# A projection phase and an expert phase on one core: batch 0's attention chain issued one projection step sooner, two edits at the start, and fourteen filling matmuls taken out

## The reference, cut to what matters

```
h = layernorm(x) * (1 + ca) + sa
Q, K, V = h @ Wq.T + bq, h @ Wk.T + bk, h @ Wv.T + bv        # 16 heads of 16
Q, K = elu(Q) + 1, elu(K) + 1
KV, K_sum = einsum('bshd,bshe->bhde', K, V), K.sum(axis=1)    # over the whole batch
Z = 1 / (einsum('bshd,bhd->bsh', Q, K_sum) + 1e-06)
x = x + ga * (einsum('bshd,bhde,bsh->bshe', Q, KV, Z) @ Wo.T + bo)
h = layernorm(x) * (1 + cb) + sb
gates = softmax over the best 2 of 8 of (cosine(h, centroids) + h @ w_route.T)
x = x + gb * sum over experts of gates * (gelu(h @ w1 + b1) @ w2 + b2)
```

## Time and profile before

| | us |
|---|---|
| median of 3 runs | 363.19 (362.65 to 363.71) |
| the profiled execution, own time | 362.67 |
| its span | 360.9 |
| PE busy | 346.5 (96%) |
| DVE busy | 286.6 (79%) |
| POOL busy | 259.4 (72%) |
| ACT busy | 234.7 (65%) |

### The profile page before, as it was taken

One profiled execution on the slowest core, in us unless ns is written; L12 is line 12 of the kernel. 1 busy time (PEld: TensorE's weight loads), 2 busy tenths in 40 slices (PEclk: granted clock), 3 DMA queues, 4 the chain that ended last, 5 costly groups with the idle time before them and its releaser, 6 DMA issues.

```text
span 360.9 us, 8816 instructions
## 1 busy us (share of the span) xinstructions
PE 346.5 (96%) x2790; PEld 324.3 (90%) x2790; DVE 286.6 (79%) x819; ACT 234.7 (65%) x517; POOL 259.4 (72%) x358
## 2 busy tenths in 40 slices
PE   8899999998999988799999999999999999999995
PEld 8667888887888977799998999999999999999895
DVE  5589676658748889989999889898898888876754
ACT  4685878887877745756747476584574765855541
POOL 4367999977867587787897878988889867755210
PEclk9999999999999999999999999999999999999999
DMA  8953630000000033133242322421323214214311
GB/s 266 331 167 94 192 96 0 2 3 0 2 0 3 4 117 119 56 93 105 55 136 80 69 91 61 147 85 63 130 65 97 88 60 145 91 61 145 98 51 61
DMA packets 23715, 31.82 MB, mean 88 GB/s; under 512 B 2288, under 2 KB 14204, under 8 KB 23680
## 3 DMA queue, kind: packets, MB, share of 16 engines
q1 hardware_dynamic: 23240, 31.34, 28.2%
q10 hardware_dynamic: 440, 0.04, 0.1%
HBM read 27.04 MB, written 4.34 MB: 87 GB/s over the span
## 4 chain that ended last, share of the span: by engine, by line
PE 73%; DVE 17%; issue 4%; ACT 3%; DMA 1%; POOL 1%; DVEq 0%; ACTq 0%; POOLq 0%
PE bank L797 20%; PE bank L798 19%; PE bank L799 19%; PE bank L805 4%; PE bank L852 3%; DVE hid_g L1355 2%; PE bank L829 2%; PE bank L981 2%; DVE bank L1372 2%; DVE early L1272 1%; DVE gT_f L1411 1%; DVE den L1303 1%; PE bank L1023 1%; PE bank L908 1%; DVE qz_lo L1310 1%
## 5 line engine op out<-in xcount | busy, mean ns | idle before, releaser
L740 ACT ACTIVATE bank<-bank,cols_sb 128x256 f32<-128x256 f32 x128 | 51.3, 438 | 43.3 <-PE bank L799 43.0
L797 PE MATMUL bank<-tr_hi,w_hi 128*128 128x256 f32 x256 | 73.4, 287 | 0.0
L798 PE MATMUL bank<-tr_lo,w_hi 128*128 128x256 f32 x256 | 72.3, 282 | 0.0
L799 PE MATMUL bank<-tr_hi,w_lo 128*128 128x256 f32 x256 | 72.1, 282 | 0.0
L797 PE MATMUL bank<-w_hi,hid_pair 128*128 128x256 f32 x252 | 70.5, 280 | 0.0
L799 PE MATMUL bank<-w_hi,hid_pair 128*128 128x256 f32 x252 | 70.3, 279 | 0.0
L798 PE MATMUL bank<-w_lo,hid_pair 128*128 128x256 f32 x252 | 70.2, 279 | 0.0
L501 POOL TENSOR_TENSOR hid_pair<-hid_g,hid_pair 128x512 fp32r<-128x512 f32 x42 | 54.3, 1292 | 7.0 <-POOL gT_r L526 3.3
L797 PEld LDWEIGHTS bank<-tr_hi,w_hi 128*128 128x128 f32 x256 | 48.8, 191 | 0.3 <-DVE hid_g L1355 0.2
L799 PEld LDWEIGHTS bank<-tr_hi,w_lo 128*128 128x128 f32 x256 | 48.9, 191 | 0.0
L798 PEld LDWEIGHTS bank<-tr_lo,w_hi 128*128 128x128 f32 x256 | 48.8, 191 | 0.0
(11 more groups left out here) (162 smaller groups left out, 928.3 us busy)
## 6 DMA issues: line engine op xcount, KB each, us to landing
g_bc<-g_dram SPq DMA_DIRECT2D x64, 256.0 KB, 3.5
x_sb<-in_x SPq DMA_DIRECT2D x16, 256.0 KB, 3.0
out<-x_sb SPq DMA_DIRECT2D x15, 256.0 KB, 2.3
early<-in_wmod SPq DMA_DIRECT2D x3, 512.0 KB, 7.0
q_sb<-in_w SPq DMA_DIRECT2D x2, 512.0 KB, 6.5
q_sb<-in_w SPq DMA_DIRECT2D x1, 1024.0 KB, 9.5
mod_row<-mod_dram SPq DMA_DIRECT2D x1, 1024.0 KB, 6.2
q_sb<-in_wqkvT SPq DMA_DIRECT2D x2, 384.0 KB, 5.3
```

Source lines behind the costliest of these rows:

```text
L740: last = ac.activation(half, half, ACT.Gelu, bias=b1_sb[:, e:e + 1])
L797: te.matmul(out_ap, l_hi, r_hi, start=start, stop=False, skip_group_check=shared)
L798: te.matmul(out_ap, l_hi, r_lo, start=False, stop=False, skip_group_check=shared)
L799: return te.matmul(out_ap, l_lo, r_hi, start=False, stop=stop, skip_group_check=shared)
```

## The change

In words, engine by engine:

- Start: VectorE makes the low half of the bias row (`bqk_r`) ahead of unit 0's low half, not behind it. TensorE issues `v(0)` ahead of `tp_a(1)`.
- TensorE, projection phase: `sum_k(0)` from inside step 9 to the end of step 8; `make_m(0)` from inside step 11 to the end of step 10; `tp_o(0)` and `tp_o(1)` from steps 12 and 14 to 11 and 13; `attend(0)` and `attend(1)` from 13 and 15 to 12 and 14; `tp_e(0)` and `route(0)` from step 15 and behind it to step 14.
- The other engines move their parts of it in the same way. New in step 15 are, on VectorE, `gates_a(0)` ahead of the feature map of the first half of unit 15 and `gates_b(0)` between the two halves; on GpSimd `exp_gates(0)`, then `rstd_e(1)`, then `add_bo(7)`; on ScalarE `normalise_e(1)` ahead of `keep_v(15)`.
- Step -1: TensorE issues `first(0, 0)`, `kv(15)`, `first(0, 1)`, `tp_e(1)`, `first(0, 2)`, `tp_o(2)`, `first(0, 3)`, `attend(2)`, `sum_k(1)`, `route(1)`; both fills are gone. ScalarE does `square(1)` and `hi_e(1)` between the first two gelus. `tp_o(2)` now waits for unit 1's low half (`e_lo` one higher), since both use bank 0.

```diff
@@ POOL step_a
-                if u.nth(UPB + 6):
+                if u.nth(UPB + 5):
                     rstd_e(unit(0))
...
+                if u.nth(NU - 1):
+                    exp_gates(unit(0))
+                    rstd_e(unit(1))
+                    add_bo(unit(UPB - 1))
@@ ACT step_a
+                if u.nth(NU - 1):
+                    normalise_e(unit(1))
                 if u.plus(2):
                     normalise(u.plus(2))
-                if u.nth(UPB + 4):
-                    hi_o(unit(0))
                 keep_v(u)
@@ PE step_a
                 if u.nth(NU - 1):
                     kv(u.plus(-1))
                 v(u)
+                if u.nth(0):
+                    tp_a(u.plus(1))
                 if u.plus(-1) and not u.nth(NU - 1):
                     kv(u.plus(-1))
+                if u.nth(UPB):
+                    sum_k(0, bank[0][:, 0:E])
+                if u.nth(UPB + 2):
+                    make_m(0, bank[1])
+                if u.nth(UPB + 6):
+                    pe.wait_ge(route_ready, 1)
+                    route(unit(0))
@@ PE step_e
+                if u.nth(-1):
+                    first(u.plus(1), 1)
+                    tp_e(unit(1))
+                    first(u.plus(1), 2)
                 if u.plus(3):
                     tp_o(u.plus(3))
...
-                    fill(bank[6], 7)
@@ DVE, the start
+            dve.wait_ge(bqk_step, 2)
+            TT(bqk_r[32:33, :], bqk_raw[32:33, :], bqk_t[32:33, :].bitcast(F32), ALU.subtract).then_inc(bqk_ready, 1)
             dve.wait_ge(a_hi, 1)
             TT(tr_lo[:, 0, :, :], tr_f[:, 0, :, :], tr_hi[:, 0, :, :].bitcast(F32), ALU.subtract).then_inc(a_lo, 1)
@@ DVE step_a
                 if u.nth(NU - 1):
 
                     dve.wait_ge(w_ready, NU)
+                    gates_a(unit(0))
...
                 feature_map(u, 0)
                 if u.nth(NU - 1):
-                    lo_e(unit(0))
-                    add_attention(unit(1))
+                    gates_b(unit(0))
                 feature_map(u, 1)
```

More of the change, by code:

```diff
@@ L531, in step_e @@
                     lo_e(u, 0)
-                if u.plus(1):
+                if u.plus(1) and not u.nth(-1):
                     exp_gates(u.plus(1))
@@ L753, in step_e @@
                     gelu(u.plus(1), 0)
+                    square(unit(1))
+                    hi_e(unit(1))
+                    gelu(u.plus(1), 1)
                 if u.plus(3):
@@ L761, in step_e @@
                     gelu(u, 1)
-                if u.nth(-1):
-                    gelu(u.plus(1), 1)
-                if u.plus(2):
+                if u.plus(2) and not u.nth(-1):
                     normalise_e(u.plus(2))
@@ L857, in step_a @@
                 qk(u, 0)
-                if u.nth(NU - 1):
+                if u.plus(1) and not u.nth(0):
+                    tp_a(u.plus(1))
+                if u.nth(UPB + 3):
+                    tp_o(unit(0))
+                if u.nth(UPB + 5):
+                    tp_o(unit(1))
+                qk(u, 1)
+                if u.nth(UPB + 4):
+                    attend(unit(0))
+                if u.nth(UPB + 6):
                     attend(unit(1))
                     tp_e(unit(0))
[L861 to L875, removed]
                 if u.nth(NU - 1):
@@ L1063, in step_e @@
                 if u.nth(-1):
-                    for p in range(1, NP):
-                        first(u.plus(1), p)
+                    first(u.plus(1), 3)
                 if u.nth(0):
@@ L1082, in step_e @@
                     second(u, 0)
+                if u.plus(2) and not u.nth(-1):
+                    tp_e(u.plus(2))
                 if u.nth(-1):
                     pe.wait_ge(a_acc, NU + 1)
-                    fill(bank[6], 7)
[L1086 to L1089, removed]
                     sum_k(1, bank[6][:, 0:E])
@@ L1429, in step_e @@
                     keep_ksum(1, bank[6][:, 0:E])
-                if u.plus(1):
+                if u.plus(1) and not u.nth(-1):
                     gates_a(u.plus(1))
                 if u.nth(-1):
-                    stats_e(unit(1))
+                    modulate_e(unit(1))
                     add_kv(unit(NU - 1))
+                    denominators(u.plus(4))
+                    lo_e(unit(1))
                 if u.nth(5):
```

83 lines of the change are left out of this document (39 added, 44 removed).

## The result

The changed kernel takes 364.02 us (median of 16 runs, 363.26 to 364.35), the kernel before 363.22 (16 runs). The ratio is 1.0019, 95% interval 1.0012 to 1.0026: a loss of 0.8 us by the medians, small but clear of the noise, where 0.1 was forecast. The time lies in the range of 361.6 to 364.7, and the forecast of no change beyond 0.3% held. The profiled execution of the changed kernel took 363.50 us, its span 361.8 (before 360.9).

The account below looks back on a forecast made before the run. Bound: TensorE's position through projection, then VectorE's start of gate(0,0). Terms -0.1 - 1.0 + 0.8 + 0.5 + 0.5 + 0.4 + 0.4 - 1.4 = +0.1 on 362.67 gave 362.8, as a median 363.3 us; range 361.6 to 364.7.

Parts of the forecast that it names:

- What bounds: Up to the projection phase's end TensorE's position counts, then when VectorE begins gate(0,0); that instruction's shift is the forecast.
- The start: From the first operations to qk(1,0): a gain of 0.1 us, qk(1,0) at 20.0 instead of 20.11.
- My lower bound: At the start: a loss of 0.1 us if the low half's later start slows the chain.
- sum_k and make_m: End of steps 8 and 10: sum_k(0) waits for GpSimd's add_ksum, +0.8 us; make_m(0) no longer waits, -1.0 us.
- the rival of a late place_kv: Step 10: make_m also waits, place_kv behind a locked mask_kv; 0.5 of the 1.0 returns, 363.8 us; chance 0.08.
- Step 14 and kv(15): TensorE waits for unit 14's low half on GpSimd, +0.5 us, and before kv(15) in step 15, +0.5 us.
- the two branches: Before kv(15): VectorE's gates_b and feature map ready at 119.6; GpSimd and ScalarE through keep_v(15) at 120.4; both needed.
- Step -1: Bridge to the expert phase: tp_o(2) waits for lo_e(1), +0.4 us; tp_e(1) ahead of attend(2), +0.4; shorter tail, -1.4.
- The tail: From the start of attend(2) to gate(0,0): 3.5 us instead of 4.87, -1.4 us.
- the faster rival: Steps 14, 15 and -1: the new waits of 0.5, 0.5 and 0.4 don't come; 361.9 us; chance 0.27.
- The gates holding up unit 15: VectorE and ScalarE in step 15: late gates_a(0) delays kv(15); decides from about 1.2 us more, 364.8 with 1.5; chance 0.17.
- The clock: TensorE: 3 us of matmuls at 1.2 GHz instead of 2.4 would cost 3 us more, 366 us; chance 0.02.

## Why the prediction came out as it did

**What bounds (held, with a wrong reason).** The forecast was the shift of gate(0,0), and it was: from there to the end of the span lie 231.15 to 231.6 us in every kernel in which gate(0,0) kept its place. The reason given, VectorE's unbroken sequence, was only a part of it. With the gates sooner VectorE was relieved of 1.28 us and the end did not follow, since GpSimd's sequence had come later; with the fills out most of the 0.55 us was gone again by tp_e(3).

**The start (failed, +0.57 for -0.1).** The chain was followed to qk(1,0), where it was right within 0.2 us, and dropped there. Behind it, unit 1's later high half (18.04 against 17.58, 0.46) makes GpSimd and VectorE late up to unit 3's high half. VectorE itself had caught up to 0.18 by 27.68, but GpSimd's centroid norms were 0.64 late, VectorE waited for them, and TensorE met the 0.64 in step 3, where it had no slack. My lower bound, a loss of 0.1, had left this out. The bias edit was priced on the wrong side as well: ahead of qk(0,0), where I put 0.2, it cost 0.3 in this execution and 0.1 to 0.5 in others, but with the transposes first it gained 0.7 to 0.8 behind.

**sum_k and make_m (held).** +0.87 at kv(8) for +0.8; the wait before make_m is gone, and kv(7) to kv(10) came out 0.2 above the forecast, with unit 0's transposes moved into it. The 1.1 us more put on VectorE for mask_kv did not come either: its two operations took 0.92 us at 79.05, not 2.08, and with that the rival of a late place_kv is out.

**Step 14 and kv(15) (nearly held).** The waits were 0.35 and 0.83 us, 1.2 for 1.0; over the stretch +0.77, for unit 1's transposes had moved ahead of it. kv(15) waited for VectorE (feature map and add_kv(14), 120.62) and for keep_v(15) (120.55) alike, as the two branches said.

**Step -1 (held).** It came out at -0.51 for -0.6. The tail is 3.49 for 3.5. The wait before tp_o(2) was 0.2, not 0.4: lo_e(1) ended at 124.88 and the transposes began at 125.02, where the matmul ahead of them would have let them begin at 124.79. attend(3) waits 1.40 and first(1,0) 0.75, for the 2 us put at attend(3).

**Rivals.** The new waits all came, so the faster rival is out. The gates holding up unit 15 was the right place, but the wait was 0.83 us, 0.3 more than the 0.5 put there; 1.2 more was to decide. The clock did not fall.

Some luck is in the small total. The start was missed by 0.67 us, and 0.2 of too much at steps 14 and 15 took a part of that back. Within the start two errors met: the order of v(0), from which I expected some 0.3 us (the 0.1 and the bias edit's 0.2), cost 1.1 in the trace, and the bias edit, put at a cost, saved 0.8. Without that saving the loss would have been nearer 1.6 us; this assumes that the two add, which no run shows.

## What to carry to other kernels

When an edit fills a wait of the busiest engine by letting something go later, follow the delayed result down the queue of every engine that handles it, for as many steps as units are worked on ahead, and not only to its first reader: here a high half that came 0.46 us late in step 0 came back as 0.64 us, and as a wait of 0.81 on TensorE, three steps on. A small operation put into an engine's idle time can pay through what then stands directly behind the critical one; it also uses up the slack that hid a late input ahead of it. And before an operation is moved up against its producer, look at the producer's queue: one swap on GpSimd was worth 0.9 us.

## What the runs showed of the hardware

- Even a tiny VectorE operation can be held for a whole GpSimd one: 128x16 with two inputs in SBUF took 1.25 us beside add_ksum and 0.17 otherwise. The Trainium skill ("SBUF — State Buffer", "Who interferes with whom") says that such a pair excludes each other for the whole instruction; the trace agrees, and shows that here the small one lost as much (1.1 us) as a 128x256 one (1.38 for 0.43).
- 3.9 us of idle TensorE in 22 us, in pieces up to 1.3 us, left the granted clock at 1.00, 2.4 GHz.
- The start of the first projection matmul differs between the profiled executions by over 1 us (11.33 to 12.65), and all the late ones are kernels with the bias edit. VectorE's first weight split waited 1.58 us for its DMA before and 2.63 in the execution that starts at 12.65. How much of the spread of the medians this makes is not shown.
